# A graph network's kernel: part of the gathers as one-hot products on TensorE, the layer norm's stages rewritten, and the attention's end joined with the stage behind it

## The reference

```python
# L0: three graph convolutions, weighted sum over the edges into dst
h = x @ fc_w[l].T + fc_b[l]; m = f[src] * edge_w; agg = segment_sum(m, dst)
# L1: edge convolution, maximum over the edges into dst
e = relu((x[dst] - x[src]) @ theta.T + theta_b + x[src] @ phi.T + phi_b)
out = segment_max(e, dst)
# L2: attention with 8 heads of 32; every node has an edge to itself as well
e = leaky(e_left[src] + e_right[dst]); alpha = softmax over the edges into dst
out = segment_sum(Wh[src] * alpha, dst)
# L3, three layers: maximum over the edges out of src, then batch norm and relu
e = relu((x[dst] - x[src]) @ thetas[l].T + x[src] @ phis[l].T)
agg = segment_max(e, src); x = relu(batchnorm(agg) * gammas[l] + betas[l])
```

## Time and profile before

| | |
|---|---|
| median of 3 runs | 4944.62 us (4943.63 to 4951.45) |
| the profiled execution | 4944.8 us, its span 4943.0 us |
| busy: POOL, DVE | 3310.2 us (67%), 3029.2 us (61%) |
| busy: PE, PE weight loads, ACT | 1524.9 us, 1035.0 us, 1032.3 us |
| POOL's gathers in the seven edge passes (L1290) | 2744 of 968 and 964 ns |
| DMA | 898 MB, 182 GB/s over the span |

### The profile page before, as it was taken

The page is one execution under the profiler, slowest core; times in us unless marked ns, Lnnn a source line. Parts: engine busy times, 40 slices in busy tenths (PEclk is TensorE's granted clock), DMA queues, the critical chain, the costliest instruction groups (busy, mean ns, idle before and its releaser), DMA issues. The chain is left out here.

```text
span 4943.0 us, 34587 instructions
## 1 busy us (share of the span) xinstructions
PE 1524.9 (31%) x7148; PEld 1035.0 (21%) x7148; DVE 3029.2 (61%) x9035; ACT 1032.3 (21%) x2614; POOL 3310.2 (67%) x3435
## 2 busy tenths in 40 slices
PE   6221075556655566444520001400006000330004
PEld 5110053334433343111220001300006000230003
DVE  5897565556656568888868888733334333433335
ACT  3333334443444432000121112200002000010002
POOL 3777747776577755777657775077775777657774
PEclk8555575555655577666675555755558555665556
DMA  2656536665466633656446664156653666455663
GB/s 88 227 196 223 205 122 206 206 213 180 149 206 206 209 112 125 202 203 204 160 124 220 217 220 158 37 205 209 210 199 130 206 210 208 158 172 206 207 208 120
DMA packets 270260, 898.04 MB, mean 182 GB/s; under 512 B 69883, under 2 KB 106088, under 8 KB 226024
## 3 DMA queue, kind: packets, MB, share of 16 engines
q0 software_dynamic: 161760, 439.40, 30.6%
q1 hardware_dynamic: 108296, 456.51, 23.5%
HBM read 449.86 MB, written 445.80 MB: 181 GB/s over the span
## 5 line engine op out<-in xcount | busy, mean ns | idle before, releaser
L1290 POOL DMA_INDIRECT WORK<-table,SRCI x1568 | 1518.3, 968 | 639.5 <-issue 494.0
L1290 POOL DMA_INDIRECT WORK<-table,BYSRC x1176 | 1133.9, 964 | 558.2 <-issue 396.9
L1339 DVE SCALAR_TENSOR_TENSOR WORK<-WORK,LOWE 128x256 f32<-128x256 f32 x1564 | 761.7, 487 | 967.5 <-DMA WORK<-table,BYSRC 879.3
L1339 DVE SCALAR_TENSOR_TENSOR WORK<-WORK,NST,e_mv 128x256 f32<-128x256 f32 x1173 | 563.2, 480 | 498.9 <-issue 225.0
L1309 ACT ACTIVATE e_mv<-WORK,WE 128x256 f32<-128x256 f32 x1176 | 491.2, 463 | 836.9 <-DMA WORK<-table,SRCI 803.1
L990 PE MATMUL bn_ps<-ident,WORK 128*128 128x128 f32 x6 | 2.0, 434 | 1478.1 <-PEq L148 1478.1
L1644 POOL DMA_INDIRECT WORK<-table_attention,SRCI x392 | 374.4, 955 | 119.6 <-issue 119.6
L1421 ACT ACTIVATE WORK<-bn_ps 128x256 f32<-128x256 f32 x3 | 1.2, 384 | 1483.3 <-PE bn_ps L1001 1483.3
L990 PEld LDWEIGHTS bn_ps<-ident,WORK 128*128 128x128 f32 x6 | 0.9, 203 | 1479.2 <-issue 1479.2
L961 PE MATMUL e_hi<-ARENA 128*128 128x392 bf16 x392 | 188.2, 480 | 265.3 <-DVE ARENA L947 265.3
L897 PE MATMUL e_rb<-ARENA 98*128 98x128 bf16 x392 | 114.6, 292 | 441.7 <-ACT ARENA L913 441.7
(11 more groups left out here) (355 smaller groups left out, 4363.6 us busy)
## 6 DMA issues: line engine op xcount, KB each, us to landing
edge_results<-WORK SPq DMA_DIRECT2D x343, 1024.0 KB, 4.4
edge_results_attention<-WORK SPq DMA_DIRECT2D x98, 544.0 KB, 3.2
WORK<-table,SRCI POOLq DMA_INDIRECT x1568, 2.8
table<-ARENA SPq DMA_DIRECT2D x35, 640.0 KB, 3.2
WORK<-table,BYSRC POOLq DMA_INDIRECT x1176, 2.8
WORK<-table_attention,SRCI POOLq DMA_INDIRECT x392, 3.2
table_attention<-ARENA SPq DMA_DIRECT2D x5, 660.0 KB
X<-in_x SPq DMA_DIRECT2D x4, 640.0 KB
```

What stands on the lines that cost most here:

```text
L1290: eng.indirect_dma_start(G[:, q * GT + k, 0:D], None, T, bass.IndirectOffsetOnAxis(ap=index[:, t:t + 1], axis=0)).then_inc(got[q].sem, 16)
L1339: eng.scalar_tensor_tensor(O[:, q % OB, k, :], behind, mask[:, ds(g * GT + k, 1)], here, op0, op1).then_inc(linked, 1)
```

## The change

- `edge_pass` has a list `picks`. For e5, e6 and e7 it names 28 of the 98 groups (g = 0, 4, 7, 11, ... 95). In these POOL fetches three tiles instead of four. The fourth is made on the core: DVE spreads the tile's node numbers on a diagonal (`lay_out`, 7 groups ahead), PE sums it over the partitions, DVE compares the numbers with 5 x 5 node tiles (`one_hots`, 5 groups ahead: five operations of 640 elements, one input in PSUM), and PE sums 25 products of one-hot tiles with the table's copy in AGG (128x128 by 128x256, float32). DVE links from PSUM and waits for `used`.
- e3 gets 12 sets of slots (`DEEP`), the further six in AGW_BASE. L1's own term moves from n4 into e3 (`all_beside`), with the bias as a third product; n4 keeps its turned tiles in C. The own term of L3's first layer moves from n6 to e5. Turned tiles now lie in C (view CT) instead of YT, also in batch norm.
- Norm stages n4 and n5: `apply` on DVE ends with the shift. The normalized row is written once, by ACT's `keep` into X, which now waits for the factors and counts `staged`; PE turns X. ACT's order becomes `square_root` 3, `keep` 2, `ahead` 1, `behind` 0; DVE's order stays.
- `attention_nodes` takes the place of comb and n6: one selector operation per tile (256 elements, ring of 13), PSUM ring of 3 instead of 4, leaner scores; of the three products and sums of a chunk, one product and one sum go to POOL, behind its 25 gathers; DVE keeps two products and two sums, and waits for POOL ahead of its last sum. Then bn_stats, the factors, ACT's rows, PE's turns and the product with TH3[0] follow chunk by chunk, and SP stores the table.

```diff
@@ node_products @@
                     def apply(t, slot, _):
                         eng.wait_ge(rooted, t + 1)
-                        eng.wait_ge(kept, t + 1)
+                        if t >= u:
+                            eng.wait_ge(staged, t - u + 1)
                         eng.reciprocal(factor[:, slot:slot + 1], root[:, slot:slot + 1]).then_inc(factors, 1)
                         eng.wait_ge(factors, t * 2 + 1)
                         eng.tensor_scalar(shift[:, slot:slot + 1], MV5[:, slot, 0:1], factor[:, slot:slot + 1], -1.0,
                                           ALU.mult, ALU.mult).then_inc(factors, 1)
-                        eng.wait_ge(factors, t * 2 + 2)
-                        eng.wait_ge(turned, t + 1)
-                        eng.tensor_scalar(R[:, slot, :], tile_of(X, t), factor[:, slot:slot + 1], shift[:, slot:slot + 1],
-                                          ALU.mult, ALU.add).then_inc(staged, 1)
...
                     def keep(t, slot, _):
-                        eng.wait_ge(staged, t + 1)
+                        eng.wait_ge(factors, t * 2 + 2)
                         eng.activation(tile_of(X, t), tile_of(X, t), ACT.Identity,
-                                       bias=shift[:, slot:slot + 1], scale=factor[:, slot:slot + 1]).then_inc(kept, 1)
+                                       bias=shift[:, slot:slot + 1], scale=factor[:, slot:slot + 1]).then_inc(staged, 1)
...
-                        pipelined(NT, u, eng, (square_root, 3), (ahead, 1), (keep, 1), (behind, 0), flat=True)
+                        pipelined(NT, u, eng, (square_root, 3), (keep, 2), (ahead, 1), (behind, 0), flat=True)
@@ edge_pass @@
+            sets = SETS if weighted or picks else DEEP
+            pick_of = {g: i for i, g in enumerate(picks)}
+            CH, BITS = 5, NT // 5
...
-                        for k in range(GT):
+                        for k in range(GT - (g in pick_of)):
                             t = g * GT + k
-                            eng.indirect_dma_start(G[:, q * GT + k, 0:D], None, T,
+                            eng.indirect_dma_start(slot(g, k), None, T,
...
+                    def spread_nodes(i):
+                        if i < len(picks):
+                            eng.wait_ge(laid, i + 1)
+                            if i >= 2:
+                                eng.wait_ge(hots, (i - 1) * BITS)
+                            eng.matmul(rows_ps[:, i % 2, 0:P], ones[:, :], diag[:, i % 2, :], start=True, stop=True).then_inc(spread, 1)
+                    def pick(g, q, turn):
...
+                        spread_nodes(i + 1)
+                        if i >= 4:
+                            eng.wait_ge(linked, (picks[i - 4] + 1) * GT + 8)
+                        for c in range(BITS):
+                            eng.wait_ge(hots, i * BITS + c + 1)
+                            for j in range(c * CH, (c + 1) * CH):
+                                n = P if j < NT - 1 else LAST
+                                last = eng.matmul(made_ps[:, i % 4, 0:D], hot_rows[0:n, i % 2, j, :], AGG[0:n, j, :], start=j == 0, stop=j == NT - 1)
+                            last.then_inc(used, 1)
...
+                                if k == GT - 1 and g in pick_of:
+                                    eng.wait_ge(used, (pick_of[g] + 1) * BITS)
+                                    here = made_ps[:, pick_of[g] % 4, 0:D]
...
+                    def one_hots(g, q, turn):
+                        if g in pick_of:
+                            i = pick_of[g]
+                            eng.wait_ge(spread, i + 1)
+                            for c in range(BITS):
+                                if i >= 2:
+                                    eng.wait_ge(used, (i - 2) * BITS + c + 1)
+                                at = slice(c * CH, (c + 1) * CH)
+                                eng.tensor_tensor(hot_rows[:, i % 2, at, :], rows_ps[:, i % 2, 0:P].unsqueeze(1).broadcast_to([P, CH, P]),
+                                                  key[:, at].unsqueeze(2).broadcast_to([P, CH, P]), ALU.is_equal).then_inc(hots, 1)
+                    picking = [(lay_out, 7), (one_hots, 5)] if picks else []
@@ attention_nodes, POOL @@
+                    for k in range(NT // u):
+                        eng.wait_ge(weighed, k + 1)
+                        eng.tensor_tensor(by_head(C, k), by_head(C, k), share(2, k), ALU.mult).then_inc(pooled, 1)
+                        eng.wait_ge(pooled, 2 * k + 1)
+                        eng.tensor_tensor(X[:, chunk(k), :], X[:, chunk(k), :], C[:, chunk(k), 0:D], ALU.add).then_inc(pooled, 1)
@@ attention_nodes, ACT @@
+                    square_roots(0)
+                    square_roots(1)
+                    for k in range(NT // u):
+                        eng.wait_ge(scaled_rows, k + 1)
+                        for t in range(k * u, (k + 1) * u):
+                            eng.activation(X[:, t, :], X[:, t, :], ACT.Identity, bias=NMR[:, t:t + 1], scale=RST[:, t:t + 1]).then_inc(staged, 1)
+                        for t in range(k * u, (k + 1) * u):
+                            eng.wait_ge(xturned, t + 1)
+                            eng.activation(C[:, t, 0:D], tps[:, t % 2, 0:D], ACT.Copy).then_inc(xt, 1)
+                            if 0 < t <= ONE:
+                                evict(t - 1)
+                        if k + 2 < NT // u:
+                            square_roots(k + 2)
@@ attention_nodes, DVE @@
+                    def join(k):
+                        T = chunk(k)
+                        c.inc(eng.tensor_tensor(by_head(YW, k), by_head(YW, k), share(0, k), ALU.mult))
+                        c.link(eng.tensor_tensor(by_head(AGW, k), by_head(AGW, k), share(1, k), ALU.mult))
+                        c.link(eng.tensor_tensor(YW[:, T, 0:D], YW[:, T, 0:D], AGW[:, T, 0:D], ALU.add))
+                        eng.wait_ge(pooled, 2 * k + 2)
+                        c.link(eng.tensor_tensor(X[:, T, :], X[:, T, :], YW[:, T, 0:D], ALU.add))
+                        for j in range(u):
+                            c.inc(eng.bn_stats(BS[:, j, :], X[:, k * u + j, :]))
...
+                    shares(0)
+                    join(0)
+                    scores(1)
+                    shares(1)
+                    join(1)
+                    for k in range(2, NT // u):
+                        scores(k)
+                    shares(2)
+                    factors_of(0)
+                    factors_of(1)
+                    for k in range(2, NT // u):
+                        join(k)
+                        if k + 1 < NT // u:
+                            shares(k + 1)
+                        factors_of(k)
@@ flow_l1, flow_l3 @@
-            node_products("n4", None, DF1, copy_to(AGG), TH1, out2, table=(AGG, T), norm=(add_bias,), marks=(first_src, flag_src))
-            edge_pass("e3", SRCI, (ALU.add, ALU.max), LOWE, False, order_beside)
+            node_products("n4", None, DF1, copy_to(AGG), None, nothing_else, table=(AGG, T), norm=(add_bias,), marks=(first_src, flag_src),
+                          keep_turned=True)
+            edge_pass("e3", SRCI, (ALU.add, ALU.max), LOWE, False, all_beside(order_beside, own_term_beside(TH1, B1)))
...
+        PICKS = [g for g in range(NG) if g * 28 // NG != (g - 1) * 28 // NG]
...
-                edge_pass(f"e{5 + l}", BYSRC, (ALU.add, ALU.max), LOWE, False, own_term_beside(l) if l else nothing_beside)
+                edge_pass(f"e{5 + l}", BYSRC, (ALU.add, ALU.max), LOWE, False, own_term_beside(DF3[:, l]), picks=PICKS)
```

More of the change, by code:

```diff
@@ L23 @@
 SETS = 6
+DEEP = 2 * SETS
 ET = NG * GT
@@ L1024, in node_products @@
                 if norm is not None:
-                    added, aggregated, rooted, factors, kept, apart = (
-                        st.sem(n) for n in ("added", "aggregated", "rooted", "factors", "kept", "apart"))
+                    added, aggregated, rooted, factors, apart = (
+                        st.sem(n) for n in ("added", "aggregated", "rooted", "factors", "apart"))
                     adds = len(norm) + 1 + (crossing is not None)
@@ L1341, in _ @@
+                    if picks:
+                        eng.tensor_copy(node_of[:, :], index.rearrange("p (g k) -> p g k", k=GT)[:, :, GT - 1]).then_inc(keyed, 1)
+                        eng.tensor_scalar(key[:, :], iota_b[:, 0:NT], float(P), iota_p[:, 0:1], ALU.mult, ALU.add).then_inc(keyed, 1)
+                        eng.wait_ge(keyed, 2)
+                    picking = [(lay_out, 7), (one_hots, 5)] if picks else []
                     early, late = beside_on("vector", eng)
-                    pipelined(NG, U, eng, *early, (link, 0), *late, flat=flat, head=0 if flat else U)
+                    pipelined(NG, U, eng, *early, *picking, (link, 0), *late, flat=flat, head=0 if flat else U)
@@ L1532, in batch_norm, with nothing_else, all_beside, beside @@
                 g.close(u)
-        def own_term_beside(layer):
+        def nothing_else(eng, t, slot, ps, done):
```

(28 more changed lines are left out.)

242 lines of the change are left out of this document (148 added, 94 removed).

## The result

| | before | after |
|---|---|---|
| median | 4948.03 us of 4 runs (4943.63 to 4952.42) | **4832.9 us** of 4 runs (4829.55 to 4836.04) |
| span of the profiled execution | 4943.0 us | 4833.5 us |
| busy: POOL, DVE, PE | 3310, 3029, 1525 us | 3261, 3287, 2609 us |

What follows compares the result with a forecast made beforehand. POOL's gather issue, 1.25 us each, was taken to bound the edge passes, with DVE or DVE and ACT between them. Terms -105 + 0 + 11 + 1 - 16 = -109 gave 4836 us, range 4790 to 4882.

Steps and rivals of the forecast that it cites:

- Picks: Last three edge passes: 28 gathers fewer in each, at 1.25 us, take 105 us off POOL's path; ends 60 and 108.
- the covers: Last three edge passes: PE's and DVE's work per pick fits within the 16.3 us of 13 gathers.
- The far bound: Last three edge passes: gathers beside picks could cost at most 15 us more per pass; nothing was added.
- Rival 4: Last three edge passes: picks stay on a cold PE, +120 us each, +360 in all, 5200 us; chance 0.04.
- Rivals 3 and 5: Last three edge passes: picks pay 60 us, total 4881, chance 0.15; or don't shorten passes, total 4941, chance 0.03.
- e3: Edge pass with L1's own term: twelve sets give nothing, own term hidden beside PE work; 0 us, bounds -3 and +5.
- The loop in n5: Norm stage: ACT's `keep` and DVE's factors wait for each other in a row; step 3.8 us, +11 us.
- Rival 2: Both norm stages: no loop, steps shrink by DVE's savings, -25 in place of +12, total 4800 us; chance 0.08.
- n4: Norm stage: step 2.6 us against 2.47, +3, less 2 for `out2` and products gone: +1 us.
- The joined stage: Comb and the norm stage behind it made one: the new chain ends at 3179 against 3194.7, -16 us.
- Turns: Joined stage: DVE's products with two SBUF inputs and POOL's alternate, so POOL's part adds; a join 13.9 us.
- Rival 1: Joined stage: POOL's part is wholly hidden, -32 in place of -16, total 4820 us; chance 0.15.

Runs made afterwards that it cites:

- the run with lead 3: Changed kernel with only DVE's `apply` one step earlier in the norm stages (lead 3 in place of 2): 4789.04 us, 0.9677 of before.
- The early exponential: ACT's exponential of chunk 0 behind tenth fill, third product and sum on DVE, against changed kernel: 5922.21 us beside 5883.32; with `apply` lead 3 and 35 picks: 4760.07 us.

## Why the prediction was right

- **Picks** (-105, measured -101.2). The time of a gather on POOL's queue was the right price, and the covers held: a pick 11.15 us on PE (10.5 warm was forecast) or 12.3 to 13.9 (12.8 from cold), five comparisons 3.75 on DVE (4.0). Without the picks the passes get their 100.5 us back. The 4 us missing are two things: a pass took 1.268 us per gather before (1491.5 by 1176), not 1.25, which makes the 84 worth 106.5; and it took 1.273 beside picks, which takes back 5.3 over the 1092 that are left. A gather had been forecast to cost no more beside picks. The far bound named there, e3's 15 us per pass, was not near. Rival 4 was in part there: about half of the picks ran in part at a clock of 0.50. But none stayed there (0.88 to 0.89 over the pass), and at most 13.9 us a pick is under the 17.5 from which that rival counts. Rivals 3 and 5 fell by the size.
- Two slips in that part. Rival 4's price of 5200 adds its +360 to the forecast of 4836, which has the picks' 105 taken off already; +120 a pass counts from the kernel before, so it should have read about 5300. And "a PE without gaps is granted 1.00" holds for the stretch in the earlier trace rows, but not in general: in the joined stage PE was busy without a gap for 28 us at 0.50 (last section).
- **e3** (0, measured -0.1), and six sets are as good as twelve.
- **The loop in n5** (+11, measured +12.3): step 3.8 forecast, 3.77 measured. Rival 2 fell, and the run with lead 3 shows the cause by itself. **n4** (+1, measured +0.2): step 2.6 forecast, 2.66 measured in its second half. The net was right, but my "+3, less 2" is not the price of either half of the edit: the work moved out is worth -11.5 by itself and the loop costs 11.7. That two amounts so much larger than my terms cancel to +0.2 is luck as far as the terms go. I had not asked for the two apart, and so did not see what opening the loop would be worth.
- **The joined stage** (-16, measured -18.7): first share to end 108.8 us forecast (3070.2 to 3179), 106.2 measured, with the first share 46.5 us behind the start of the stage in both kernels. POOL's pair is 2.35 + 2.88, where 5.6 was set. Turns were the right rule: 1280-element instructions of 3.7 to 4.2 us. The Trainium skill ("GPSIMD Engine Reference", Key points) names the shared SBUF interfaces; the trace agrees with it, as 1.49 became 3.68 and 4.16. Rival 1 fell: it had POOL's part hidden, and taking that part away gains 9 to 14 us.
- What the forecast did not have: that the stretch ahead of the first share changes from run to run (that it "stays" held only in this profile). In five other profiles, of kernels whose joined stage is the same, that stage took 157.7 to 166.7 us, which is -18 to -9. So that this term came within 3 us owes something to the run that was profiled. And the total, 3 us beside the median, is nearer than its terms: the picks saved 4 us less than forecast, all other stages together 4 more.

## What to carry to other kernels

Here a gather left out was worth its time on the issuing queue as long as every other engine's period per replaced gather, with the side work of that stretch in it, was shorter; the mean over the pass is not enough, as 35 picks showed. When an engine's step is shortened, look at the order in which two in-order queues wait for each other: here one digit, the lead of `apply`, was worth 44 us, while the leaner step as first written was 23 us slower than the old one in the same kernel. A second engine on the same memory should be priced by turns before it is called help: here two fewer instructions on DVE cost more than they saved.

## What the runs showed of the hardware that I had not expected

**TensorE's clock in the joined stage differs from run to run.** Between the first selector and the first share PE crosses over the chains, tile after tile, and ACT's exponential stands behind it. The table by stretch of 4 us, first the changed kernel, then the one without picks, whose program is the same up to there:

```profile
3066.37:3070.37 4.00, 4.00 (x26) 3.61 (x25) 3.25 (x13) 3.28 (x13) 3.08 (x4) 1.00 0.38 104
3070.37:3074.37 4.00, 4.00 (x26) 3.61 (x25) 2.25 (x7) 3.28 (x13) 3.08 (x4) 1.00 0.37 104
```

```profile
3072.88:3076.88 4.00, 4.00 (x13) 3.38 (x13) 2.99 (x9) 1.72 (x7) 3.09 (x4) 0.50 0.40 109
3076.88:3080.88 4.00, 4.00 (x13) 3.36 (x13) 1.04 (x3) 1.72 (x8) 3.09 (x4) 0.50 0.41 114
```

At a granted clock of 1.00 (2.4 GHz) PE starts 26 records in 4 us, at 0.50 (1.2 GHz) 13, and ACT's fills go with them. In the first kernel the clock rose early in the crossing, in the second it did not rise at all, though PE had no gap in either: from 3064.84 to 3092.84 us it was busy for all 28.00 us, at 0.50. From first selector to first share it was 20.0 us in the one and 34.2 in the other (27.1 in the run with the third product on DVE, where the clock rose in the middle). No edit made these 14 us. How much of them counts depends on what waits behind them. The row of the stage without picks:

```profile
3036.32:3202.99 166.67, 72.49 (x254) 57.96 (x255) 110.95 (x231) 46.90 (x139) 52.50 (x36) 0.59 0.19 62
```

It is 9.4 us longer than in the changed kernel, not 14: there DVE stood 10 us in chunk 0 for POOL's gathers and sum, and a later first share first uses up that wait; then POOL's part falls beside DVE's first two products, which take 3.32 and 4.16 us instead of 1.49. With the third product on DVE no such wait exists, and the 7.1 us of that run counted in full. Either is more than some edits are worth. The early exponential should take most of it off the path, as chunk 0 then waits for the fills of ten tiles and not of 25; its one run at the usual time had a clock that rose early, so this is not shown.

**DVE is held even where it moves almost nothing.** L2052, 5 elements, took 0.17 us alone and 2.0 to 2.6 beside POOL's 1280-element instructions.
